# Moving two sums and the inverse from VectorE to GpSimd, and splitting unit 0's sums in a graph-attention kernel

## The reference

```python
h = jnp.einsum('bnf,hfo->bhno', x, W)
s1 = jnp.einsum('bhno,ho->bhn', h, a1)
s2 = jnp.einsum('bhno,ho->bhn', h, a2)
e = jax.nn.leaky_relu(s1[..., :, None] + s2[..., None, :], negative_slope=0.2)
attn = jax.nn.softmax(jnp.where(adj > 0, e, -9e15), axis=-1)
h_prime = jnp.einsum('bhnm,bhmo->bhno', attn, h)     # heads side by side: (b, n, 512)
x = layernorm(x + h_prime)
```

## Time and profile before

| what | value |
|---|---|
| time, median of 3 runs | 2842.45 us (2840.01 to 2843.44) |
| the profiled execution | 2844.84 us, its span 2843.1 us |
| TensorE busy | 2667.5 us (94% of the span) |
| VectorE busy | 2491.9 us (88%) |
| ScalarE busy | 2333.0 us (82%) |
| GpSimd busy | 1236.4 us (43%) |
| mean granted clock of TensorE | 0.978 of full speed |

### The profile page before, as it was taken

One profiled execution on the slowest core, in us unless ns is written; L12 is line 12 of the kernel. 1 busy time (PEld: TensorE's weight loads), 2 busy tenths in 40 slices (PEclk: granted clock), 3 DMA queues, 4 the chain that ended last, 5 costly groups with the idle time before them and its releaser, 6 DMA issues.

```text
span 2843.1 us, 126766 instructions
## 1 busy us (share of the span) xinstructions
PE 2667.5 (94%) x52546; PEld 2313.9 (81%) x52546; DVE 2491.9 (88%) x3836; ACT 2333.0 (82%) x3886; POOL 1236.4 (43%) x1011
## 2 busy tenths in 40 slices
PE   6899999999999999999999999999999999999996
PEld 3499876999679986799958999499984999859986
DVE  6799988889898998999889998889988999889996
ACT  4599974999659997599957998489983999839994
POOL 4544436434354434544354443544436444264442
PEclk9999999999999999999999999999999999999998
DMA  6456643676535765277553775447754477546773
GB/s 186 101 132 166 164 127 90 135 167 154 137 78 140 173 148 146 69 151 177 136 135 76 175 171 133 117 99 170 168 122 115 113 165 167 124 107 127 165 169 94
DMA packets 281214, 390.33 MB, mean 137 GB/s; under 512 B 161857, under 2 KB 161857, under 8 KB 280673
## 3 DMA queue, kind: packets, MB, share of 16 engines
q1 hardware_dynamic: 253536, 315.24, 42.5%
q0 software_dynamic: 27136, 67.12, 14.4%
HBM read 313.52 MB, written 34.14 MB: 122 GB/s over the span
## 4 chain that ended last, share of the span: by engine, by line
PE 53%; ACT 22%; issue 9%; DVE 9%; DMA 3%; POOL 2%; SPq 1%; DVEq 0%; ACTq 0%; POOLq 0%
ACT m_pos L630 19%; PE ps L549 18%; PE ps L518 10%; PE ps L583 10%; PE ps L584 10%; ACT adj_cut L595 2%; DMA y<-in_x 1%; PE ps L429 1%; PE ps L466 1%; DVE m_pos L849 1%; DMA adj_in<-in_adj 1%; PE ps L448 1%; PE ps L479 1%; DVE m_pos L835 1%; DVE prod L818 1%
## 5 line engine op out<-in xcount | busy, mean ns | idle before, releaser
L630 ACT ACTIVATE m_pos<-ps,s_steep 128x512 fp8e4<-128x512 f32 x3432 | 2063.0, 952 | 119.6 <-DVE s_neg L789 62.8
L583 PE MATMUL ps<-d_hi,m_neg 128*128 128x65 f16 x16384 | 1081.1, 194 | 19.2 <-issue 18.8
L584 PE MATMUL ps<-d_lo,m_neg 128*128 128x65 f16 x16384 | 1079.2, 194 | 14.0 <-issue 13.5
L584 PEld LDWEIGHTS ps<-d_lo,m_neg 128*128 128x128 fp8e5 x16384 | 1028.1, 98 | 62.9 <-issue 31.2
L549 PE MATMUL ps<-b_both,m_pos 128*128 128x130 f16 x16384 | 1016.6, 221 | 53.9 <-DVE total L692 20.3
L583 PEld LDWEIGHTS ps<-d_hi,m_neg 128*128 128x128 fp8e5 x16384 | 1043.4, 98 | 18.3 <-issue 18.0
L549 PEld LDWEIGHTS ps<-b_both,m_pos 128*128 128x128 fp8e5 x16384 | 962.2, 98 | 63.4 <-issue 62.5
L1011 POOL TENSOR_TENSOR den_scaled<-den_inv,bound 128x4 f32<-128x4 f32 x256 | 506.5, 1979 | 1120.9 <-DVE den_inv L703 1104.8
L849 DVE TENSOR_TENSOR m_pos<-m_pos,maskT 128x1024 uint32<-128x1024 uint32 x512 | 620.1, 1228 | 146.8 <-ACT m_pos L630 145.2
L856 DVE TENSOR_TENSOR m_neg<-m_pos,maskT 128x2048 uint32<-128x2048 uint32 x256 | 586.6, 2291 | 1.1
L518 PE MATMUL ps<-W_sb,xT 128*128 128x512 f32 x1024 | 455.0, 605 | 32.6 <-issue 20.9
(11 more groups left out here) (94 smaller groups left out, 1563.5 us busy)
## 6 DMA issues: line engine op xcount, KB each, us to landing
adj_in<-in_adj SPq DMA_DIRECT2D x266, 512.0 KB, 4.7
s_bc<-s_rows SPq DMA_DIRECT2D x258, 256.0 KB, 3.6
x_in<-in_x SPq DMA_DIRECT2D x134, 256.0 KB, 4.4
x_sum<-in_x POOLq DMA_DIRECT2D x128, 256.0 KB, 4.9
y<-in_x POOLq DMA_DIRECT2D x32, 1024.0 KB, 9.8
out<-y SPq DMA_DIRECT2D x32, 1024.0 KB, 6.6
maskT<-adj_cut SPq DMA_TRANSPOSE x264, 4.1
m_neg<-in_x SPq DMA_DIRECT2D x10, 256.0 KB, 3.1
```

Of the source, the lines that this page charges most:

```text
L583: pe.matmul(acc, mask, d_hi[:, j, h, :], start=(j == 0), stop=False)
L584: mm = pe.matmul(acc, mask, d_lo[:, j, h, :], start=False, stop=(j == JC - 1))
L630: ins = nc.scalar.activation(chunk(m_pos[unit % 3], j, 0, BLK), ps[:, BANK_S1 + unit % 2, :], ACT.Relu, bias=s2_steep[:, j, h:h + 1], scal ...
```

## The change

GpSimd takes over the sum of the two parts (`total += neg_part`) and the inverse of the denominator, which becomes a power of -1. VectorE's `take_neg` ends after the product, which goes to one of two `neg_part` buffers. The compares stay where they are. In unit 0, TensorE does `m_pos` chunks 0 to 11, then `m_neg` chunks 0 to 12, then `m_pos` chunks 12 to 15, `spread_s1` of unit 3, the transposes, and `m_neg` chunks 13 to 15. The third bank of `H_BANKS` becomes 3, and the projection's third chunk waits for `neg_read` of unit 31. `mean_part` lies in `prod_d`.

```diff
-    H_BANKS = (7, 6, 2)
+    H_BANKS = (7, 6, 3)
...
+    POS_FIRST, NEG_FIRST = 12, 13
...
-                        pe.wait_ge(neg_read, at(neg_read, b * UNITS - 1))
+                        pe.wait_ge(neg_read, at(neg_read, b * UNITS))
...
+                        if unit == 0:
+                            pe.wait_ge(mean_made, b + 1)
+                            pe.wait_ge(pos_made, at(pos_made, QUADS * (u + 1)))
...
+                            pe.wait_ge(lo_made, at(lo_made, 2 * JC * b + 2 * POS_FIRST - 1))
...
+                            add_pos(unit, h, 0, POS_FIRST)
...
+                            add_neg(h, range(IT), 0, NEG_FIRST)
+                            pe.wait_ge(lo_made, at(lo_made, 2 * JC * (b + 1) - 1))
...
+                            mm = add_pos(unit, h, POS_FIRST, JC)
+                            mm.then_inc(pos_summed, 1)
+                            spread_s1(3, u + 3)
+                            turn_x(JC * (b + 1), x_in[0][:], x_loaded[0], b * (JC // 2), 0)
+                            pe.wait_ge(lo_made, at(lo_made, 2 * JC * (b + 1)))
...
+                            mm = add_neg(h, range(IT), NEG_FIRST, JC)
+                            mm.then_inc(unit_done, 1)
...
-                V.tensor_tensor(neg_part[:], neg, r, ALU.mult).then_inc(neg_read, 1)
-                dve.wait_ge(neg_read, at(neg_read, u + 1))
-                V.tensor_tensor(total[hp][:], total[hp][:], neg_part[:], ALU.add).then_inc(total_made, 1)
-                dve.wait_ge(total_made, u + 1)
-                V.reciprocal(den_inv[hp][:], total[hp][:, :, O]).then_inc(den_inverted, 1)
+
+                V.tensor_tensor(neg_part[hp][:], neg, r, ALU.mult).then_inc(neg_read, 1)
...
+                pool.wait_ge(pos_read, at(pos_read, u + 1))
+                pool.sem_inc(waited[pool.engine], 1)
+                pool.wait_ge(neg_read, at(neg_read, u + 1))
+                G.tensor_tensor(total[hp][:], total[hp][:], neg_part[hp][:], ALU.add).then_inc(total_made, 1)
+                pool.wait_ge(total_made, u + 1)
+                G.tensor_tensor(den[hp][:], total[hp][:, :, O], minus_one[:], ALU.pow).then_inc(den_inverted, 1)
                 pool.wait_ge(den_inverted, u + 1)
-                G.tensor_tensor(den_scaled[hp][:], den_inv[hp][:], bound[:].to_broadcast([P, IT]), ALU.mult
+                G.tensor_tensor(den_scaled[hp][:], den[hp][:], bound[:].to_broadcast([P, IT]), ALU.mult
```

More of the change, by code:

```diff
@@ L481, in mean_h, with add_pos, add_neg @@
                 mm.then_inc(h_mean_summed, 1)
+            def add_pos(unit, h, first, last):
+                for it in range(IT):
+                    acc = slot(0, it)
+                    for j in range(first, last):
+                        mask = chunk(m_pos[unit % 3], j, it * P, P).bitcast(FP8_WIDE)
+                        mm = pe.matmul(acc, mask, b_both[:, j, h, :, :], start=(j == 0 and it % 2 == 0),
+                                       stop=(j == JC - 1 and it % 2 == 1))
+                        if j == 0:
+                            pe.matmul(acc[:, 0:O1], tiny_bf[:], mean[:, h, :], start=False, stop=False)
+                return mm
+            def add_neg(h, tiles, first, last):
+                for it in tiles:
+                    acc = ps[:, 2 + h % 2, it * O1:(it + 1) * O1]
+                    for j in range(first, last):
+                        mask = chunk(m_neg[h % 2], j, it * P, P).bitcast(FP8_WIDE)
+                        pe.matmul(acc, mask, d_hi[:, j, h, :], start=(j == 0 and it == 0), stop=False)
+                        mm = pe.matmul(acc, mask, d_lo[:, j, h, :], start=False, stop=(j == JC - 1 and it == IT - 1))
+                return mm
             pe.nop().then_inc(x_turned, start[x_turned])
@@ L537, in _ @@
                             pe.sem_inc(waited[pe.engine], 1)
[L538 to L552, removed]
+                            mm = add_pos(unit, h, qd * JQ, (qd + 1) * JQ)
                         mm.then_inc(pos_summed, 1)
-                        if unit == 0:
-                            pe.wait_ge(lo_made, at(lo_made, 2 * JC * (b + 1)))
                         if unit == STAT_UNIT + 1:
@@ L792, in batch_start @@
             def batch_start(b):
+                dve.wait_ge(neg_read, at(neg_read, UNITS * b))
+                dve.sem_inc(waited[dve.engine], 1)
                 dve.wait_ge(exp_made, b + 1)
@@ L1027, in _ @@
             G.memset(minus_half[:], -0.5)
+            G.memset(minus_one[:], -1.0)
             G.memset(x_sum[:], 0.0)
```

40 lines of the change are left out of this document (22 added, 18 removed).

## The result

The changed kernel takes 2856.99 us (median of 7 runs, 2849.94 to 2861.57). The kernel before, beside it on the same chip, took 2842.45 us. The ratio is 1.0045, with an interval of 1.003 to 1.0061: slower by 13 us, where I had predicted 13 us faster. The spans of the two profiled executions differ by less, 2852.7 and 2843.1 us. In all seven runs of the changed kernel the time is 4.2 to 4.5 us more than the span, and 1.7 to 1.8 us in the kernel before: 2.6 us of the loss lie outside the span, where no trace shows them.

A forecast was written before the change was run, and what follows sets the result against it. Four engines were 81% to 94% busy; ScalarE set the pace through most units, its restart moving the batch. 26 - 4 - 8 - 1 = 13 us off 2844.84 gave 2831.8, less 2.4 for the median: 2829.5 us, range 2814 to 2850.

The forecast's parts named there:

- Part 1, unit 0: Unit 0 of each batch: the new order starts ScalarE's compares of unit 3 earlier, gaining 26 us, bounds 15 and 30.
- I take it as full: Unit 0's start, 4 us earlier, was assumed to reach the end of the batch undiminished.
- Part 2, VectorE's relief: Lines 701 and 703 hold VectorE 0.57 us a unit; removing them is worth nothing where VectorE waits for ScalarE.
- Part 3, what GpSimd does to VectorE: Every unit: GpSimd's product and scaling can hold VectorE 0.5 to 0.8 us against 0.57 saved; net taken as 0.
- Part 4, the middle of the batch: Unit 18: VectorE waits about 3 us for the residual's transfer in most batches; 0.5 us a batch, 4 us lost.
- Part 4, the end of a batch: Unit 30: take_pos waits 1.1 us longer for GpSimd's `y` at 7 boundaries, 8 us lost; bounds 0 and 2.3 each.
- The residual's wait in full: Unit 18: 3.3 us of waiting, TensorE waiting behind it until the batch's end; 26 us, not 4; 2851.5 us; chance 0.13.
- The power holding VectorE: Every unit: GpSimd's power holds VectorE too, 0.9 us a unit net, 45 us in all, 2874 us; chance 0.05.

The follow-up runs named there:

- the order alone: Changed kernel with its new order of unit 0, but VectorE adds and inverts as before: 2820.52 us, ratio 0.9937; run again later 2819.24 us, ratio 0.9916.
- The experiment with more compares: 16 more compares a batch moved from ScalarE to VectorE, in two kernels: 2816.6 us with GpSimd adding except units 28 and 29, 2806.51 us with VectorE adding.
- the second trace: The changed kernel run once more, later, with nothing altered: 2850.18 us, ratio 1.0041.
- The kernel with the later exclusive-or: Changed kernel plus a spare VectorE sum and reciprocal in unit 28, GpSimd still making all real ones: 2839.5 us, ratio 0.9997.
- the one that also spares GpSimd the two units' sums: Changed kernel with VectorE adding and inverting in units 28 and 29 only: 2827.68 us, ratio 0.9955.
- the one with two powers: Changed kernel in which GpSimd takes every unit's power twice, the first into a spare place: 2880.82 us, ratio 1.0146.

## Why the prediction was wrong

**Part 1, unit 0, held.** 26 us were predicted for the stage, 27.3 measured (8 x 3.41), the start 8.26 us after the first sum where I said 8.7, and the clock no longer fell. "I take it as full" is less sure: alone the new order brought 18 to 24 us by the ratios, and some 21 by the medians, though its two spans are 30 and 26 us shorter than the profiled one of before. The few us between are not settled.

**Part 2, VectorE's relief, held**, and more firmly than put. The relief is 119 us and the added waiting 118, and in the order alone, without the relief, the wait is 145.9 us as before. The experiment with more compares shows that they did not need it either.

**Part 3, what GpSimd does to VectorE, was too high.** GpSimd's sum takes 0.72 us when free and 2.71 in the median, where I had said 0.6 and 2.8. For what holds VectorE I said 0.5 to 0.8 us a unit, from one AND of 1.37 us. Measured is what the ANDs gained over the kernel before (1228 to 1248 ns, 512 times: 10 us) and the compares (483 to 512 ns, 664 times: 20 us), 30 us over 256 units or 0.12 us a unit. The row was stretched by 0.15 us; I took the whole length of product and scaling for every unit, where most products fall between VectorE's instructions. Only half of the compares' 20 us lies beside the products (30 of them, 0.36 us each). The other half lies beside GpSimd's issuing of its transfers and its clearing of `x_sum`, where a compare took up to 1.14 us; this I had not priced at all. It did not matter for the sum, which had the net at zero. That the power does not hold VectorE was right; pairs of ANDs of 3.4 us because of it did not come.

**Part 4, the middle of the batch, failed in its mechanism.** The wait of 3 us for the residual in unit 18 is not there: line 729 waits once in the whole trace, at the kernel's end, for 12.1 us (in the second trace three times, 13.9 us in all, 12.2 of them at the end). A cost came in another place, the 1.0 to 1.8 us a batch of adjacency pieces, which no rival named. I took 4 us and the traces have 9 to 15.

**Part 4, the end of a batch, is the step that failed.** I put 1.1 us at 7 boundaries, with bounds of 0 and 2.3; it is 3.5 us in the mean of the eight ends (19.28 less 15.74), 28 us where the sum had 8. (Some 5 us of them, 2 in the second trace, are made up again before the next batch's first sum.) VectorE does wait for `y` behind GpSimd's return, as I wrote. With the exclusive-or held back, so that the reduction is short as before, the path to unit 30 grows by 1.3 us and TensorE's end by 1.0, close to my 1.1. The term missed a piece. I wrote that the wait grows "by 1.67 less the 0.57 us by which VectorE gets out of the way earlier". That 0.57 us was not a relief but the cause of the larger half. The exclusive-or that begins 0.6 us earlier falls ahead of the reduction and blocks it for 1.7 us; before, the reduction was 0.21 to 0.73 us ahead. I had described the same exchange for line 1011 in Part 3 and did not carry it to the reduction, whose margin the trace of before shows. The kernel with the later exclusive-or puts 2.5 of the 3.5 us on this, and the one that also spares GpSimd the two units' sums brings back the rest. The Trainium skill's figure of about 6 us (page "GPSIMD Engine Reference", section "Instruction dispatch") is not what GpSimd's return takes: that is 7.0 to 9.4 us in all traces.

**The sum.** Predicted -26 + 4 + 8 + 1 = -13. From the first trace -27 (unit 0) + 15 (unit 3 to 18) + 28 (ends) - 6 (all other stages) = +10, the difference of the spans 2852.7 and 2843.1. Most of the -6 is a shorter stretch from TensorE's last sums to its first of the next batch. With the 2.6 us outside the span this comes to +12; the ratio gives +13.

**The rivals.** The change came out slower, but by none of them. The residual's wait in full (2851.5) had the nearest time and the wrong place. The power holding VectorE (2874) is refuted twice. The slower ones priced GpSimd's added time in the middle of the batch, where it costs at most 1 to 2 us, and not behind the reduction. My range ended at 2850, just short of the residual's case, and the bound of 2.3 us at an end was never added to it: 7 x 1.2 = 8 us more would have held the result, by a microsecond and for the wrong reason.

## What to carry to other kernels

A microsecond taken off an engine also moves everything behind it, so look at what the next instructions come into contact with, and with what margin: here 0.6 us saved on VectorE turned an order of 0.45 us between two engines around and cost 1.7 us on the path. Price an addition to a helper engine at the one place in the loop where somebody waits for it, and divide the work there otherwise: two units of 32 put back were worth 26 of the 31 to 36 us that the move costs on top of the new order. And where an engine already waits 145 us for another, relieving it buys waiting; the useful step was the opposite one, more work for it (16 compares a batch, some 8 to 11 us).

## What the runs showed of the hardware that I had not expected

- A partition reduction on GpSimd is short itself (0.42 us) but GpSimd is unavailable around it: 5.7 to 6.7 us (once 8.1) from the last maximum to its start, and 7.0 to 9.4 us from its end to the next instruction, in every kernel here. Some 14 to 18 us pass from that maximum to its next instruction, with little but the reduction in them. In seven batches of the changed kernel some 2 us of these come from VectorE's exclusive-or ahead of it.
- A GpSimd power over 128 x 4 elements takes 1.02 to 1.06 us when nothing holds it and does not lengthen VectorE's ANDs. A product over 128 x 256 of 0.61 us lengthens a VectorE compare that begins during it from 0.48 to 0.84 us, and an AND from 1.22 to up to 1.64.
- Useless work of 0.61 us on VectorE, once in each batch, made the changed kernel some 14 us faster.
- A kernel's time outside its profiled span is not the same in all kernels here: 4.2 to 4.5 us in every run of the changed kernel and of the four others in which GpSimd adds, and 1.7 to 1.8 us in every run of the kernel before, of the two in which VectorE adds, and of the one with two powers. No run shows why.
